# A three-stage graph layer on one core: the rows for routing and experts stay 32-bit until their transpose has left PSUM

## The reference, cut to what matters

```
xn  = layernorm(x)
x   = x + gcn(gcn(xn)) + linear_attention_block(xn)
f   = layernorm(x)
out = x + ffn(f)

ffn(f):
  logits = f @ router_w.T                  # 8 experts
  probs  = softmax(logits); top_w, top_i = top_k(probs, 2)
  e_sel  = max(top_i)                      # the larger index of the best two
  out[row] = silu(f[row] @ w1[e_sel]) @ w2[e_sel]      # 768 -> 128 -> 768
```

## Time and profile before

| | |
|---|---|
| median of 3 runs | 2583.36 us (2581.44 to 2583.81) |
| span of the profiled execution | 2579.3 us |
| that execution's own time | not given; its span lies 4.1 us under the median of the runs |
| TensorE matmul / weight load busy | 2372.9 us (92%) / 1607.5 us (62%) |
| VectorE, ScalarE, GpSimd busy | 1304.3 us (51%), 872.7 us (34%), 817.4 us (32%) |
| mean granted TensorE clock | 0.964 of 2.4 GHz |
| second graph layer with routing | about 2010 to 2433 us of the span |
| expert tiles | 2449 to 2579 us of the span |

### The profile page before, as it was taken

The page is one execution under the profiler, slowest core; times in us unless marked ns, Lnnn a source line. Parts: engine busy times, 40 slices in busy tenths (PEclk is TensorE's granted clock), DMA queues, the critical chain, the costliest instruction groups (busy, mean ns, idle before and its releaser), DMA issues.

```text
span 2579.3 us, 45374 instructions
## 1 busy us (share of the span) xinstructions
PE 2372.9 (92%) x16783; PEld 1607.5 (62%) x16783; DVE 1304.3 (51%) x2843; ACT 872.7 (34%) x1323; POOL 817.4 (32%) x565
## 2 busy tenths in 40 slices
PE   3899889999899999998899999999998899999576
PEld 2686768787666666665565566666664556666365
DVE  5464547564476766766313444544441334444444
ACT  2353436454474654745112222222220001111033
POOL 0002103656677777877610000000000000000265
PEclk9889899999899999999999999999998999999799
DMA  9698977664423233132543999999986655444287
GB/s 389 243 404 286 400 274 247 165 164 115 99 2 62 11 52 61 0 62 7 130 103 110 295 289 302 278 303 274 283 269 237 210 195 173 171 160 157 73 171 129
DMA packets 192199, 474.24 MB, mean 184 GB/s; under 512 B 74864, under 2 KB 81882, under 8 KB 182460
## 3 DMA queue, kind: packets, MB, share of 16 engines
q1 hardware_dynamic: 109996, 381.82, 40.6%
q0 software_dynamic: 71264, 61.03, 18.0%
q10 hardware_dynamic: 10800, 29.50, 3.0%
HBM read 266.99 MB, written 210.77 MB: 185 GB/s over the span
## 4 chain that ended last, share of the span: by engine, by line
PE 71%; ACT 8%; DVE 8%; DMA 6%; issue 4%; SPq 3%; POOL 0%; DVEq 0%; ACTq 0%; POOLq 0%
PE pair L1833 30%; PE pair L372 27%; PE pair L1665 4%; PE pair L1595 2%; PE pair L1645 2%; DVE arena L1297 2%; DVE arena L1299 2%; DVE arena L1303 2%; ACT arena L902 2%; DMA arena<-in_w_qkv 1%; DMA arena<-in_w_proj 1%; PE pair L1977 1%; PE pair L1964 1%; SPq L386 1%; DMA arena<-ahl_dram 1%
## 5 line engine op out<-in xcount | busy, mean ns | idle before, releaser
L372 PE MATMUL pair<-arena 128*128 128x384 f16 (+2 forms) x5760 | 912.9, 320 | 53.4 <-ACT arena L845 29.0
L711 POOL DMA_INDIRECT cells<-arena x392 | 653.5, 1667 | 626.6 <-DMA cells<-arena 501.1
L1833 PE MATMUL pair<-arena 128*128 128x384 f16 x4900 | 819.6, 328 | 27.2 <-DMA arena<-ahl_dram 12.9
L372 PEld LDWEIGHTS pair<-arena 128*128 128x128 f16 (+1 forms) x5760 | 569.5, 99 | 380.2 <-issue 57.3
L1833 PEld LDWEIGHTS pair<-arena 128*128 128x128 f16 x4900 | 475.6, 98 | 337.2 <-issue 14.6
L741 POOL DMA_INDIRECT slots<-arena x25 | 28.9, 1155 | 493.9 <-DVEq L1521 461.3
L1665 PE MATMUL pair<-arena 128*128 128x66 f32 x1200 | 165.3, 283 | 4.6 <-ACT arena L862 4.2
L1665 PEld LDWEIGHTS pair<-arena 128*128 128x128 f32 x1200 | 154.7, 201 | 13.2 <-ACT arena L862 11.0
L862 ACT ACTIVATE arena<-pair,arena 128x256 f32<-128x256 f32 x300 | 124.0, 473 | 60.9 <-PE pair L1645 58.3
L1764 PE MATMUL pair<-arena 128*128 128x320 f32 x480 | 135.2, 435 | 0.0
L1752 PE MATMUL pair<-arena 128*128 128x320 f16 x720 | 113.9, 303 | 19.7 <-DVEq L1306 15.4
(11 more groups left out here) (198 smaller groups left out, 2431.6 us busy)
## 6 DMA issues: line engine op xcount, KB each, us to landing
cells<-arena SPq DMA_DIRECT2D x50, 1600.0 KB, 16.6
arena<-cells SPq DMA_DIRECT2D x25, 1600.0 KB, 10.6
arena<-cells POOLq DMA_DIRECT2D x25, 1600.0 KB, 13.4
ahl_dram<-arena SPq DMA_DIRECT2D x25, 1600.0 KB, 14.1
arena<-ahl_dram SPq DMA_DIRECT2D x25, 1600.0 KB, 7.7
arena<-in_x SPq DMA_DIRECT2D x70, 384.0 KB, 5.2
arena<-key_dram SPq DMA_DIRECT2D x28, 896.0 KB, 5.9
split_w<-arena SPq DMA_DIRECT2D x32, 384.0 KB
```

Source lines behind the costliest of these rows:

```text
L372: ins = nc.tensor.matmul(dst[half], left(k, a), right(k, b, half), start=start and n == 0, stop=stop and n == 2)
L711: nc.gpsimd.indirect_dma_start(cells[k], bass.IndirectOffsetOnAxis(ap=idx_all[:, m:m + 1], axis=0), val_all[:, m:m + 1], None, bounds_chec ...
L1833: ins = nc.tensor.matmul(pair[u][:, half, 0:HD], a[:, 0, s * P:(s + 1) * P], X[part][:, s, half * HD:(half + 1) * HD], start=(s == 0 and p ...
```

## The change

The normalised rows are no longer split before they are stored and transposed. `fn` becomes two 32-bit buffers, `fhl` goes, and ScalarE stores `fn[u]` itself in `fn_dram` (the same 3072 bytes a row). The transposes are of 32-bit blocks, against a 32-bit identity (`ident32`, one more GpSimd instruction at the start), 6 where there were 12, and their output fills 768 columns of 32 bits over both banks of a pair. The split now comes when they leave PSUM: ScalarE copies as 16-bit, and then VectorE subtracts that copy from PSUM. The logits move to bank 5, behind the 768th column (`FREE` = 256). In the expert tiles the transposes alternate between pairs 0 and 1, so `rows_turn(j)` waits for tile j-2 instead of j-1; `up` moves to banks 4 and 5; `down` has only pair 3 and waits for the result of the tile just before.

```diff
-        fn = at(RW + 4 * D, D)
-        fhl = [at(RW + 5 * D + D * u, 2 * D, dt=F16) for u in range(2)]
+        fn = [at(RW + 5 * D + D * u, D) for u in range(2)]
+        turned = lambda i: pair[i][:, :, :].rearrange("p a b -> p (a b)")[:, 0:D]
+        FREE = D - 512
@@ GpSimd, constants
+            made.link(nc.gpsimd.tensor_copy(ident32, ident))
@@ ScalarE
-                nc.scalar.copy(rT[0], bank16(4)[:, 0:D]).then_inc(ev_hi, 1)
+                nc.scalar.copy(rT[0], turned(2)).then_inc(ev_hi, 1)
@@ layer2
-                if reused(i):
-                    act.wait_ge(xn_st[u], 16 * (13 - u) + 16 * i)
-                    act.wait_ge(tr_done, n - 1)
-                nc.scalar.copy(fhl[u][:, 0:D], fn).then_inc(hi_ready, 1)
-                act.wait_ge(lo_ready, T + n + 1)
-                act.dma_start(hl_dram[bass.ds(n * P, P), :], fhl[u]).then_inc(xn_st[u], 16)
+                act.dma_start(fn_dram[bass.ds(n * P, P), :], fn[u]).then_inc(xn_st[u], 16)
@@ rows_evict, silu
-                nc.scalar.copy(fT[0][j % 2], bank16(0)[:, 0:D]).then_inc(fT_hi, 1)
+                nc.scalar.copy(fT[0][j % 2], turned(j % 2)).then_inc(fT_hi, 1)
-                nc.scalar.activation(hact[j % 2], bank(2 + j % 2)[:, 0:P], ACT.Silu).then_inc(f_act, 1)
+                nc.scalar.activation(hact[j % 2], bank(4 + j % 2)[:, 0:P], ACT.Silu).then_inc(f_act, 1)
@@ VectorE, normal
-                if reused(n):
-                    dve.wait_ge(hi_ready, T + n)
-                cn.link(nc.vector.tensor_scalar(fn, z_out[u], ...
+                if reused(i):
+                    dve.wait_ge(xn_st[u], 16 * (13 - u) + 16 * i)
+                    dve.wait_ge(tr_done, n - 1)
+                cn.link(nc.vector.tensor_scalar(fn[u], z_out[u], ...
-            def low(n, u):
-                dve.wait_ge(hi_ready, T + n + 1)
-                nc.vector.tensor_tensor(fhl[u][:, D:2 * D], fn, fhl[u][:, 0:D], ALU.subtract).then_inc(lo_ready, 1)
             def route_evict(n):
-                dve.wait_ge(tr_done, n + 1)
-                nc.vector.tensor_copy(rT[1], bank16(5)[:, 0:D]).then_inc(ev_lo, 1)
+                dve.wait_ge(ev_hi, T + n + 1)
+                nc.vector.tensor_tensor(rT[1], turned(2), rT[0], ALU.subtract).then_inc(ev_lo, 1)
@@ rows_evict, result
-                dve.wait_ge(g_tr, j + 1)
-                nc.vector.tensor_copy(fT[1][j % 2], bank16(1)[:, 0:D]).then_inc(fT_lo, 1)
+                dve.wait_ge(fT_hi, j + 1)
+                nc.vector.tensor_tensor(fT[1][j % 2], turned(j % 2), fT[0][j % 2], ALU.subtract).then_inc(fT_lo, 1)
-                nc.vector.tensor_copy(halves(fo[j % NO]), wide(2 + j % 2)).then_inc(f_out, 1)
+                nc.vector.tensor_copy(halves(fo[j % NO]), wide(3)).then_inc(f_out, 1)
@@ TensorE
+            def turn32(i, rows):
+                for k in range(K):
+                    ins = nc.tensor.transpose(turned(i)[:, k * P:(k + 1) * P], rows[:, k * P:(k + 1) * P], ident32)
+                return ins
@@ route_turn
-                pe.wait_ge(lo_ready, T + n + 1)
+                pe.wait_ge(xn_ready, T + n + 1)
-                turn(bank16(4), bank16(5), fhl[u][:, 0:D], fhl[u][:, D:2 * D]).then_inc(tr_done, 1)
+                turn32(2, fn[u]).then_inc(tr_done, 1)
@@ rows_turn, up, down
-                if j:
-                    pe.wait_ge(fT_hi, j)
-                    pe.wait_ge(fT_lo, j)
-                turn(bank16(0), bank16(1), g_in[q][:, 0:D], g_in[q][:, D:2 * D]).then_inc(g_tr, 1)
+                if j >= 2:
+                    pe.wait_ge(fT_lo, j - 1)
+                turn32(j % 2, g_in[q]).then_inc(g_tr, 1)
-                        ins = nc.tensor.matmul(bank(2 + u)[:, 0:P], ...
+                        ins = nc.tensor.matmul(bank(4 + u)[:, 0:P], ...
-                if not isinstance(j, int) or j >= 2:
-                    pe.wait_ge(f_out, j - 1)
+                if j:
+                    pe.wait_ge(f_out, j)
-                        ins = nc.tensor.matmul(pair[2 + u][:, half, 0:HD], a[u], ...
+                        ins = nc.tensor.matmul(pair[3][:, half, 0:HD], a[u], ...
```

More of the change, by code:

```diff
@@ L102, in build @@
         y_dram = dram("y_dram", [NP, D])
-        hl_dram = dram("hl_dram", [NP, 2 * D], F16)
+        fn_dram = dram("fn_dram", [NP, D])
         slots = dram("slots", [SLOTS, 1], I32)
@@ L141, in build @@
         ident, ident_end = small(P, dt=F16), small(P, dt=F16)
+        ident32 = small(P)
         iota = small(P, dt=F16)
@@ L240, in build @@
         lnb = at(RT + 19104, 2, 16)
-        g_in = [at(RX + D * u, 2 * D, dt=F16) for u in range(NG)]
-        g_in32 = [at(RX + D * u, D) for u in range(NG)]
+        g_in = [at(RX + D * u, D) for u in range(NG)]
         FR = RX + NG * D
@@ L746, in _ @@
             for u in range(NG):
-                made.link(nc.gpsimd.memset(g_in32[u], 0.0))
+                made.link(nc.gpsimd.memset(g_in[u], 0.0))
             for u, stores in ((0, 13), (1, 12)):
@@ L756, in gather_rows @@
                 nc.gpsimd.indirect_dma_start(
-                    g_in[j % NG], None, hl_dram, bass.IndirectOffsetOnAxis(ap=ids[:, j:j + 1], axis=0),
+                    g_in[j % NG], None, fn_dram, bass.IndirectOffsetOnAxis(ap=ids[:, j:j + 1], axis=0),
                     bounds_check=NP - 1, oob_is_err=False).then_inc(gathered[j % NG], 16)
@@ L1476, in statistics2, with normal @@
                 nc.vector.tensor_scalar(lnb[:, u, 1:2], lnb[:, u, 5:6], LN_EPS, None, ALU.add).then_inc(var_ready, 1)
-            def normal(n, u):
+            def normal(n, u, i):
                 cn = Chain(dve, dve_n, 6 * n)
@@ L1498, in choose @@
                 dve.wait_ge(f_logits, n + 1)
-                ch.link(nc.vector.tensor_copy(lg, bank(4)[:, HD:HD + NX]))
-                ch.link(nc.vector.tensor_tensor(lg, lg, bank(4)[:, HD + NX:HD + 2 * NX], ALU.add))
+                ch.link(nc.vector.tensor_copy(lg, bank(5)[:, FREE:FREE + NX]))
+                ch.link(nc.vector.tensor_tensor(lg, lg, bank(5)[:, FREE + NX:FREE + 2 * NX], ALU.add))
                 ch.link(nc.vector.tensor_reduce(nmax[:, 0:1], lg, AXX, ALU.max))
@@ L1515, in place @@
                 ch.link(nc.vector.scalar_tensor_tensor(
-                    out=rjunk, in0=bank(4)[:, HD + 16:HD + 16 + NX], scalar=1.0, in1=mask16, op0=ALU.mult,
+                    out=rjunk, in0=bank(5)[:, FREE + 16:FREE + 16 + NX], scalar=1.0, in1=mask16, op0=ALU.mult,
                     op1=ALU.mult, accum_out=rank[:, 0:1]))
@@ L1530, in layer2 @@
                     choose(n - 1)
-                normal(n, u)
+                normal(n, u, i)
                 if late:
                     place(n - 1)
-                low(n, u)
             over_tiles(dve, layer2)
@@ L1542, in _ @@
             dve.wait_ge(f_prefix, T + 1)
-            ct.link(nc.vector.tensor_scalar(ntile_i, bank(4)[:, HD + 24:HD + 24 + NX], float(P - 1), None, ALU.add))
+            ct.link(nc.vector.tensor_scalar(ntile_i, bank(5)[:, FREE + 24:FREE + 24 + NX], float(P - 1), None, ALU.add))
             ct.link(nc.vector.tensor_scalar(ntile_i, ntile_i, 7, None, ALU.logical_shift_right))
@@ L1900, in route_prefix @@
             def route_prefix(n):
-                o = bank(4)[:, HD + 16:HD + 16 + NX]
+                o = bank(5)[:, FREE + 16:FREE + 16 + NX]
                 pe.wait_ge(f_mask, n + 1)
@@ L1941, in _ @@
             pe.wait_ge(f_slot, T)
-            nc.tensor.matmul(bank(4)[:, HD + 24:HD + 24 + NX], ones16, seen, start=True, stop=True,
+            nc.tensor.matmul(bank(5)[:, FREE + 24:FREE + 24 + NX], ones16, seen, start=True, stop=True,
                              skip_group_check=True).then_inc(f_prefix, 1)
```

10 lines of the change are left out of this document (5 added, 5 removed).

## The result

The changed kernel takes 2587.89 us in the median of 10 runs (2585.30 to 2590.83), the kernel before 2583.62 us in 10 runs beside it (2578.93 to 2590.45). The ratio is 1.0021, with a 95% interval of 1.0011 to 1.0031: 0.2% slower, some 3 to 8 us. The profiled execution took 2588.31 us with a span of 2586.3, 7.0 us over the span of before.

What follows compares the result with a forecast made beforehand. The prediction took TensorE's instruction list, its gap in the expert tiles included, as the bound. Its terms, 4.6 + 1.8 + 2.6 + 0.4 = 9.4 us, added to 2583.4 gave 2593 us, 0.36% slower, range 2578 to 2624.

Steps and rivals of the forecast that it cites:

- What bounds the second layer: Second layer: TensorE, busy 335.91 of 340 us, sets the time, so whatever is added to its list is paid in full.
- The price of a transpose: Each 32-bit transpose: one record of 125 ns, set by the weight load; 0.75 us a tile, 0.08 us more than before.
- Rival A: All transposes: cost like an ordinary 32-bit product, 250 ns (52 us, 2635), or 213 ns (39 us, 2622); chance 0.26.
- rival B: All transposes: a 32-bit one streams like a 16-bit one, 56 ns; -5.6 us, 2578 us, just faster; chance 0.18.
- The wait for the subtraction: Second layer: logits wait for VectorE's subtraction, which follows ScalarE's eviction; 0.20 us for each of 23 tiles, 4.6 us.
- `route_prefix` stays covered: Second layer: `choose` begins about 1.1 us later, yet its mask is ready before TensorE asks for it; no cost.
- Behind the last tile: Routing of tiles 23 and 24: transposes wait for `f_slot`, +0.7 us, and evictions run in series, +1.0; together +1.8 us.
- Expert tiles: Expert tiles: TensorE's list, gap included, is the bound, so longer transposes cost 32 x 0.08 = +2.6 us.
- The second buffer is worth nothing: Expert tiles: second PSUM buffer removes a wait that ended long before; tile 1's gain up to 0.9 us is offset, so 0.
- The end: Last expert tiles: `down(31)` waits for the copy of tile 30 in the single buffer; last add +0.4 us.
- Rival C: Second layer: longer wait for the subtraction, each 0.2 us more costing 4.6 us; 0.4 more gives 2602; within the forecast's 0.56.
- Rival D: Expert tiles: gap before `down` changes with 12 fewer TensorE instructions; 0.2 us either way is 6 us; within the forecast's 0.56.

Runs made afterwards that it cites:

- double_route: Changed kernel with each second-layer tile's six transposes made twice: 2597.41 us (one run), a tile 17.60 us against 17.07.
- probe: Changed kernel with six extra transposes per expert tile from tile 8 on (half the columns loaded, half the rows loaded, then full): 2587.23 us (one run).
- tail: Changed kernel with ScalarE evicting before it sends `z_out` and tile 24's transposes in unused pair 3: 2586.16 us, ratio 1.0003 to the kernel before.
- before_serial: Kernel before, 16-bit transposes kept, with VectorE's evictions made to wait for ScalarE's: 2587.20 us, ratio 1.0013 to the kernel before.
- one_turn: Changed kernel with a single buffer for the expert tiles' transposes: 2589.80 us, ratio 1.0019 to the kernel before.
- two_and_two: Changed kernel with two buffers each for the expert tiles' transposes and results, `up` in banks 1 and 3: 2587.47 us, ratio 1.0021 to the kernel before.

## Why the prediction was right, and where it was not

The direction, slower, and the place of the cost came true; 9.4 us of forecast stand against 4.3 between the medians, 5.4 by the ratio (2.8 to 8.0) and 7.0 in the profile. The forecast's own border between slower and the same was 5.2 us, and the result lies on it. By the profile, forecast and measured were 4.6 and 2.4 us in the second layer, 1.8 and 2.0 in the tail, 2.6 and -0.2 in the steps of the expert tiles, 0.4 and 1.4 at the end; 0.9 came from the clock and 0.4 ahead of the first transposes, neither forecast. That the sum is in the right place is in good part luck: two terms were about twice too large or not there at all, and others were missing. By the steps:

- *What bounds the second layer*: right. double_route shows that a transpose there is paid in full.
- *The price of a transpose*, 125 ns in one record: one record is right, the size was 110 ns, and the reason was wrong. I took the 129 ns of line 1654 for a load that a transpose needs as well; probe shows that streaming sets it, and that a load of 64 rows needs at most 62 ns. The 129 ns were a misreading too: they are busy time over count, and every row of ten counts its last record's own length, 0.25 us. Ten of them in the kernel before:

```profile
...
112.40 1.23 PE L1654 MATMUL pair<-arena 128*128 128x2 f32 x10
...
```

  Nine intervals in 0.98 us are 109 ns each. The term of 0.08 us a tile was nothing (0.66 against 0.67). Rival A (250 or 213 ns) and rival B (56 ns) fall with it.
- *The wait for the subtraction*: right in mechanism, 0.20 us forecast, 0.12 measured, 2.4 us over the layer instead of 4.6. The subtraction ended 3.08 us behind the start of the transposes, forecast 3.10. But I compared it with the logits' weight load, which before ran 0.16 us ahead of its product (2302.23 and 2302.39, below); in after it is 0.03 us ahead (2304.14 and 2304.17). Behind the transposes' start the loads came at 2.95 and 3.20 us, 0.25 apart, the products at 3.11 and 3.23, 0.12 apart: the lead took the rest.

```profile
...
2302.39 0.17 PE L1894 MATMUL pair<-arena 128*128 128x16 f16 x1
...
```

- *`route_prefix` stays covered*: right; the chain goes through its products without a gap.
- *Behind the last tile*, +1.8: measured +2.0, through `f_slot` (0.9 where 0.7 was forecast) and the series (1.1 where 1.0 was), as worked out. The wait for `f_slot` is confirmed by tail, the series by before_serial.
- *Expert tiles: "TensorE's list, its gap included, is the bound there too"*: this step failed. The gap is the register read, and it took up 0.66 us a step that was added to TensorE's list ahead of it (probe). My 32 x 0.08 could never have been paid. Of the 32 x 0.83 of rival A at least 32 x 0.66 = 21 us would not have been, an estimate from probe; more than 0.66 us a step was not tried with the reads in. I had named this only as what a changed gap would mean.
- *The second buffer is worth nothing*: right for the steps (one_turn); at the start it is worth about 1 us, which I had set off against the longer eviction.
- *The end*, +0.4: measured 1.4 between the adds of tiles 28 and 31. 0.55 is `down(31)` waiting, as described (two_and_two). Most of the rest is `up(31)`, which I had not looked at: it has no `rows_turn` ahead of it, so it waits for the serial eviction of tile 31, whose subtraction ends at 2570.57, and starts at 2570.78, after TensorE's weight loads had stood 0.44 us. The kernel before, at the same place, where the last transposes began at 2562.08:

```profile
...
2564.73 1.32 PE L1964 MATMUL pair<-arena 128*128 128x128 f16 x18
...
2566.01 2.37 PE L1977 MATMUL pair<-arena 128*128 x12
...
```

  From the last transposes (2562.08 before, 2567.92 after) to the last add it took 8.70 us before and 9.83 after; less 0.55, that leaves 0.6. Of it 0.2 is the later start (2.65 and 2.86 us behind the transposes) and 0.4 that the 18 products of `up(31)` then took 1.69 us instead of 1.32. Why they did is not shown. The 0.9 us at the start of the expert tiles goes with the clock, as above.
- *Rival C* (a longer wait) did not come. *Rival D* was right that the front of TensorE's list rules the steps, wrong that fewer instructions would show.
- *The Trainium skill*: its 107 ns for a load of 128 columns (page "TensorE: Matmul & The Clock Gate", section "LDWEIGHTS (loading the stationary operand)") is not what bounds here, since transposes with all 128 columns of 64 rows loaded and 64 streamed came 62 ns apart; the products of line 1654, some 110 ns apart, lie near it. Its "4× faster for FP32" (section "Terms") would be 63 ns by a quarter of 250; measured were 110, a factor of 2.3 by that count, or 2.0 by two records of 110.

## What to carry to other kernels

When two evictions that ran side by side are put in series, look at when the first one starts, not only at how long both take: an instruction or a DMA issue that was free ahead of it is now on the path, and turning that order round gave back 4 us here, 2.8 in the loop and 1.2 behind it. Before a per-step cost is multiplied by the number of steps, find out whether the step has a gap that absorbs it: the same six transposes cost 0.53 us in one stage and nothing in the other, and the cheapest way to know is to double them.

## What the runs showed of the hardware

- A 128 x 128 transpose of 32-bit numbers is one record and takes 110 ns in a row of six at the full clock, two of 16 bits 2 x 56 ns. At a granted clock of 0.50 six took 1.28 us (after, from 2459.74 to the next product at 2461.02), about twice 0.66.
- Half the loaded columns: still 110 ns (probe). Half the streamed columns and 64 rows: 62 ns apart.
- Around each read of a number from SBUF into a register of TensorE its work had a gap of some 0.9 us, and 0.66 us of transposes put ahead of the read lengthened no step: the gap shrank. Without the reads a step fell from 3.75 to 3.45 us, at a DMA share of 1.00.
- `up(31)`, which starts behind a wait, took 1.69 us for 18 products, where in the steps it takes 1.17.
